# A clamp on GpSimd with another second operation, its subtraction moved into VectorE's product, and a new written-out order on all engines

## The chip, the cores and the metric

One NeuronCore of a Trainium2 chip runs the whole program. The metric is device time in microseconds, from the launch to the end of the program.

## The reference

Input `x` is (4, 64, 24, 24). Two layers follow, each on `gn(x)` (group norm with 32 groups of 2 channels) and each added to `x`. The layers' `w_off`, `w_def` are 3x3 convolution weights.

```python
x = x + deform(gn(x), w_off, b_off, w_def, b_def)                 # layer 0
x = x + relu_groupnorm1(modulated_deform(gn(x), ...))             # layer 1
# deform: offset = conv3x3(x, w_off) + b_off        (2 numbers for each of 9 taps and each pixel)
py = base_y + ky + off_y ; px = base_x + kx + off_x
val = corner(y0, x0, wy0*wx0) + corner(y0, x0+1, wy0*wx1) \
    + corner(y0+1, x0, wy1*wx0) + corner(y0+1, x0+1, wy1*wx1)     # bilinear sample, per tap
out = einsum('bckhw,ock->bohw', val, w_def) + b_def
# layer 1 has a third number for each tap, a mask: val = val * sigmoid(mask)
```

## The kernel before, in words

The four images are two pairs. A *stage* `m` is one layer of one pair: stages 0 and 1 are layer 0 of pairs 0 and 1, stages 2 and 3 are layer 1 of the same pairs. Stage `m + 2` needs all of stage `m`; the two pairs are independent, so that one pair's arithmetic can fill the other's waits. Each stage has nine taps, and a *tap* `n = 9 m + t` (0 to 35) is the unit of the middle of a stage. A bilinear weight is a product of two tents, (min(|dx|, 1) - 1) times (min(|dy|, 1) - 1), and the sample is a small matrix product of such weights with 8x8 windows of the image.

The work of a stage, by the names that the order lists use:
- `stats`, `aggr` (VectorE), `norm` (TensorE), `group` (VectorE), `pow` (GpSimd), `normed` (VectorE): the group norm, written into `xpad`. `band` (GpSimd) copies `xpad` into `bands`; `win` (TensorE, L905, in two parts) makes the windows and `wc` (ScalarE) copies them to `xw`.
- `conv` (TensorE, L927, nine taps into one PSUM slot): the offsets. `off`, `sig` (ScalarE), `mix`, `clip`, `omax` (VectorE), `high` (ScalarE), `pos` (VectorE, L687): the positions.
- `yd`, `ym` (TensorE), `yabs`, `yh` (ScalarE), `yu`, `ymul`, `yl` (VectorE): the tents of the rows, once in a stage.
- For each tap: `x` (TensorE, L959, four matmuls) spreads the column distances into PSUM; `xabs` (ScalarE, L525) takes the absolute value into one of four `xa` buffers; `clamp` (GpSimd, L448) works on that buffer in place; `y` (TensorE, L972, eight matmuls) spreads the row tents into PSUM; `mul` (VectorE, L737) multiplies `xa` with `y`'s PSUM into the weights `s`.
- `v` (TensorE, L990, seven parts): weights times windows; it waits until the last `mul` of its stage is done. `vc` copies `v` out, by ScalarE or VectorE. `w` (TensorE, L1006, nine taps): the second convolution, which waits for all copies of its stage.
- Layer 0 ends with `mid` (VectorE, L750, residual and statistics), layer 1 with `sum`, `last`, `fmean`, `fm`, `fspread`, `fv`, `fvar`, `fpow`, `fscale`, `relu`, `fsum` and the store of `res`.
- `far` and `flag` test whether any offset is too large for the short way; a general way exists behind a branch, and the branch is read at the end of the list.

Nothing schedules at run time: `PE_ORDER`, `DVE_ORDER`, `ACT_ORDER` and `POOL_ORDER` are written-out lists, and each engine runs its list in order, waiting on semaphores. Behind an `@` in `PE_ORDER` stands the PSUM slot (0 to 3) of a job; the slot must have been read by its consumers before the next job writes it, and `xabs` of tap `n` waits for `mul` of tap `n - 4`, which frees its `xa` buffer.

In the lists before, `clip.1` stands ahead of `mul.6`, `x.9` ahead of the last parts of `v.0`, `conv.2` and then all of `v.1` behind `y.17`, and at the end all of `x.18` to `y.35` comes ahead of `v.2`, `v.3`, `w.2` and `w.3`. On GpSimd, `band.1` stands behind `clamp.1`.

Of the kernel before, what the change touches and what calls it, by code (L numbers as in the profile page):

```python
# [62 lines left out]


PE_ORDER = """
norm.0@0 conv.0.0@1 conv.0.1 conv.0.2 conv.0.3 conv.0.4 conv.0.5 conv.0.6 conv.0.7 conv.0.8 win.0.0@2
win.0.1@3 yd.0.0@0 yd.0.1@1 x.0@2 x.1@3 norm.1@0 x.2@2 x.3@0 x.4@3 y.0@1 conv.1.0@2 conv.1.1 y.1@1
conv.1.2 conv.1.3 x.5@0 conv.1.4 conv.1.5 conv.1.6 conv.1.7 conv.1.8 y.2@3 y.3@1 y.4@0 y.5@2 x.6@3 x.7@1
x.8@3 y.6@0 y.7@1 y.8@2 win.1.0@3 v.0.0@0 yd.1.0@1 yd.1.1@2 v.0.1@3 v.0.2@0 v.0.3@1 x.9@2 v.0.4@3
v.0.5@0 v.0.6@2 y.9@1 win.1.1@3 w.0.0@0 w.0.1 w.0.2 w.0.3 w.0.4 w.0.5 w.0.6 w.0.7 w.0.8 x.10@2 x.11@1  # L70
y.10@3 y.11@2 x.12@1 x.13@0 norm.2@1 x.14@3 x.15@0 y.12@2 y.13@1 y.14@3 y.15@0 x.16@2 x.17@1 y.16@2
y.17@3 conv.2.0@1 conv.2.1 conv.2.2 conv.2.3 conv.2.4 conv.2.5 conv.2.6 conv.2.7 conv.2.8 v.1.0@0
v.1.1@2 v.1.2@3 v.1.3@1 v.1.4@0 v.1.5@2 v.1.6@3 win.2.0@1 w.1.0@0 w.1.1 w.1.2 yd.2.0@2 w.1.3 w.1.4 w.1.5
w.1.6 w.1.7 w.1.8 yd.2.1@3 ym.2.0@1 x.18@2 x.19@3 ym.2.1@1 win.2.1@2 norm.3@3 x.20@0 y.18@1 y.19@2
x.21@3 x.22@0 x.23@1 y.20@3 conv.3.0@0 conv.3.1 conv.3.2 conv.3.3 conv.3.4 conv.3.5 conv.3.6 conv.3.7
conv.3.8 win.3.0@2 win.3.1@1 y.21@3 yd.3.0@0 yd.3.1@2 ym.3.0@1 y.22@3 y.23@0 ym.3.1@2 x.24@1 x.25@3
x.26@1 x.27@0 y.24@3 y.25@1 y.26@2 y.27@0 x.28@3 x.29@1 x.30@3 x.31@2 flag@1 y.28@0 y.29@3 y.30@1 y.31@2
x.32@0 x.33@3 x.34@0 x.35@1 y.32@3 y.33@2 y.34@0 y.35@1 v.2.0@3 v.2.1@2 v.2.2@0 v.2.3@3 v.2.4@1 v.2.5@2
v.2.6@0 v.3.0@3 v.3.1@1 v.3.2@2 v.3.3@0 v.3.4@3 v.3.5@1 w.2.0@2 w.2.1 v.3.6@0 w.2.2 w.2.3 w.2.4 w.2.5
w.2.6 w.2.7 w.2.8 w.3.0@3 w.3.1 w.3.2 w.3.3 fm.0@1 w.3.4 w.3.5 fv.0@0 w.3.6 w.3.7 w.3.8 fm.1@2 fv.1@1  # L80
"""

DVE_ORDER = """
stats.0.0 stats.0.1 aggr.0 group.0 stats.1.0 normed.0 stats.1.1 aggr.1 clip.0 omax.0 pos.0 yu.0.0
group.1 yl.0.0 normed.1 yu.0.1 mul.0 yl.0.1 mul.1 mul.2 mul.3 mul.4 mul.5 clip.1 mul.6 mul.7 mul.8 pos.1
omax.1 vc.0.0 yu.1.0 yu.1.1 vc.0.2 vc.0.3 yl.1.0 yl.1.1 vc.0.6 mul.9 mid.0.0 mid.0.1 aggr.2 mul.10
mul.11 group.2 mul.12 mul.13 mul.14 mul.15 normed.2 mul.16 mul.17 vc.1.0 mix.2 clip.2 omax.2 vc.1.4
vc.1.5 pos.2 yu.2.0 mid.1.0 ymul.2.0 mid.1.1 yu.2.1 aggr.3 ymul.2.1 yl.2.0 yl.2.1 group.3 mul.18
normed.3 mul.19 mul.20 mix.3 clip.3 omax.3 oall pos.3 mul.21 yu.3.0 yu.3.1 ymul.3.0 mul.22 mul.23 yl.3.0
ymul.3.1 mul.24 mul.25 mul.26 mul.27 yl.3.1 far mul.28 mul.29 mul.30 mul.31 mul.32 mul.33 mul.34 mul.35  # L90
vc.2.2 vc.2.4 vc.2.6 vc.3.1 vc.3.3 last.0.0 last.0.1 fmean.0 fspread.0 fvar.0 fscale.0 fsum.0 last.1.0
last.1.1 fmean.1 fspread.1 fvar.1 fscale.1 fsum.1
"""

ACT_ORDER = """
off.0 high.0 wc.0.0 wc.0.1 yabs.0.0 xabs.0 yh.0.0 xabs.1 yabs.0.1 xabs.2 yh.0.1 xabs.3 xabs.4 xabs.5
off.1 xabs.6 xabs.7 xabs.8 high.1 wc.1.0 yabs.1.0 yabs.1.1 vc.0.1 yh.1.0 yh.1.1 xabs.9 vc.0.4 vc.0.5
wc.1.1 xabs.10 xabs.11 xabs.12 xabs.13 xabs.14 xabs.15 xabs.16 xabs.17 off.2 sig.2 vc.1.1 vc.1.2 vc.1.3
high.2 vc.1.6 wc.2.0 yabs.2.0 yabs.2.1 xabs.18 xabs.19 yh.2.0 yh.2.1 wc.2.1 xabs.20 xabs.21 xabs.22
xabs.23 off.3 sig.3 high.3 wc.3.0 wc.3.1 yabs.3.0 yabs.3.1 yh.3.0 xabs.24 xabs.25 xabs.26 xabs.27 yh.3.1  # L100
xabs.28 xabs.29 xabs.30 xabs.31 xabs.32 xabs.33 xabs.34 xabs.35 vc.2.0 vc.2.1 vc.2.3 vc.2.5 vc.3.0
vc.3.2 vc.3.4 vc.3.5 vc.3.6 sum.2.0 sum.2.1 relu.0 sum.3.0 sum.3.1 relu.1
"""
# [1038 lines left out]
```

## Time and profile before

| | |
|---|---|
| median of 3 runs | 174.35 us (172.06 to 175.23) |
| the profiled execution | 174.54 us |
| its span | 172.7 us |
| mean granted TensorE clock | 0.84 of full |
| busy: TensorE / GpSimd / VectorE / ScalarE | 118.5 / 87.9 / 75.8 / 63.9 us |

The span is the time between the first and last instruction that the profiler saw; 1.84 us of the profiled execution lie outside it. The busy time of TensorE counts matmuls that overlap in the array by their modelled ends, so that it is no measure of how full the array is. "Start to start" below is the time from one instruction's begin to the next one's on the same engine when neither waits.

### The profile page before, as it was taken

What the parts mean: (1) busy time and instruction counts of PE and PEld (TensorE: products, weight loads), DVE (VectorE), ACT (ScalarE), POOL (GpSimd) and SP (SyncE); (2) the same over time, 40 slices, a digit from 0 to 9 for tenths busy, and PEclk for the clock granted to TensorE, in tenths of its full rate; (3) what the DMA queues carried; (4) which work ended last, traced back from release to release, by engine and by line L of the source; (5) the groups of instructions that cost most, each with busy time, mean ns of one, the idle gap of its engine ahead of it and who ended that gap; (6) DMA issues with size and microseconds to landing.
All of it is one profiled execution on the core that took longest, in us unless ns stands there. A gap on an engine that the chain in (4) does not pass through costs nothing.

```text
span 172.7 us, 4571 instructions
## 1 busy us (share of the span) xinstructions
PE 118.5 (69%) x1953; PEld 77.0 (45%) x1953; DVE 75.8 (44%) x144; ACT 63.9 (37%) x101; POOL 87.9 (51%) x64
## 2 busy tenths in 40 slices
PE   0279949861999836379999858875353769999310
...
POOL 8030099998013199990000699619999980000110
PEclk9999996999579975557999999996555599999965
...
GB/s 169 353 193 4 0 0 4 0 4 0 4 0 6 0 4 0 2 4 0 0 4 4 0 6 0 4 0 4 0 0 0 0 4 0 6 4 4 42 30 78
...
## 3 DMA queue, kind: packets, MB, share of 16 engines
...
## 4 chain that ended last, share of the span: by engine, by line
PE 41%; POOL 40%; issue 6%; DVE 4%; ACT 3%; DMA 3%; ACTq 1%; POOLq 0%; DVEq 0%
POOL xa L448 37%; PE ps L990 14%; PE ps L1006 10%; PE ps L927 8%; PE ps L905 5%; DMA full_m<-c_full 3%; ACT xa L525 1%; POOL rstd L438 1%; POOL bands L396 1%; PE ps L939 1%; DVE s L737 1%; ACT ya L506 1%; DVE xpad L665 1%; PE ps L921 1%; ACT res L544 1%
## 5 line engine op out<-in xcount | busy, mean ns | idle before, releaser
L448 POOL TENSOR_SCALAR xa<-xa 128x576 f32<-128x576 f32 x36 | 76.8, 2155 | 49.7 <-ACT xa L525 49.7
L737 DVE TENSOR_TENSOR s<-xa,ps 128x576 f32<-128x576 f32 x36 | 26.9, 753 | 36.4 <-POOL xa L448 31.1
L525 ACT ACTIVATE xa<-ps 128x576 f32<-128x576 f32 x36 | 22.6, 648 | 28.4 <-PE ps L959 20.9
L990 PE MATMUL ps<-s,xw 64*64 64x228 f32 (+5 forms) x480 | 27.6, 380 | 5.9 <-DVE s L737 5.9
L927 PE MATMUL ps<-xpad,w_o 64*64 64x288 f32 x288 | 25.1, 506 | 0.0
L990 PEld LDWEIGHTS ps<-s,xw 64*64 64x64 f32 x480 | 18.4, 142 | 14.3 <-DVE s L737 5.6
L959 PE MATMUL ps<-pos,soon 64*64 64x288 f16 x144 | 11.4, 339 | 12.7 <-DVE s L737 10.7
L533 ACT ACTIVATE val<-ps 128x504 f32<-128x504 f32 (+5 forms) x23 | 15.7, 724 | 11.3 <-PE ps L990 11.1
L972 PE MATMUL ps<-yh,soon 64*64 64x288 f16 x144 | 13.8, 364 | 8.2 <-DVE s L737 7.2
L1006 PE MATMUL ps<-val,w_d 64*64 64x288 f32 x288 | 19.3, 409 | 0.0
L927 PEld LDWEIGHTS ps<-xpad,w_o 64*64 64x64 f32 x288 | 15.4, 171 | 7.5 <-issue 5.1
L384 DVE COPY val<-ps 128x504 f32<-128x504 f32 (+5 forms) x17 | 12.5, 772 | 10.3 <-PE ps L990 10.2
L972 PE MATMUL ps<-yl,soon 64*64 64x288 f16 x144 | 14.0, 360 | 0.0
L905 PE MATMUL ps<-full_m,bands 128*64 128x64 f32 x400 | 13.0, 223 | 1.4 <-POOL bands L396 1.4
L905 PEld LDWEIGHTS ps<-full_m,bands 128*64 128x64 f32 x400 | 12.1, 138 | 3.3 <-POOL bands L396 2.0
L959 PEld LDWEIGHTS ps<-pos,soon 64*64 64x64 f16 x144 | 5.1, 109 | 18.9 <-issue 18.3
L1006 PEld LDWEIGHTS ps<-val,w_d 64*64 64x64 f32 x288 | 10.6, 132 | 5.7 <-issue 0.2
L443 POOL TENSOR_TENSOR fin<-fin,minus_half 128x1 f32<-128x1 f32 x2 | 1.1, 555 | 23.1 <-DVE fin L787 23.1
L972 PEld LDWEIGHTS ps<-yh,soon 64*64 64x64 f16 x144 | 5.9, 125 | 12.8 <-issue 11.9
L499 ACT ACTIVATE xw<-ps 128x1024 f32<-128x1024 f32 (+1 forms) x8 | 6.5, 830 | 3.5 <-PE ps L905 3.5
L474 ACT ACTIVATE off<-ps,vec 128x576 f32<-128x576 f32 x2 | 1.7, 830 | 15.4 <-PE ps L927 15.4
L477 ACT ACTIVATE off<-ps,vec 128x576 f32<-128x576 f32 x2 | 1.5, 741 | 15.4 <-PE ps L927 15.4
...
## 6 DMA issues: line engine op xcount, KB each, us to landing
...
```

Source lines behind the costliest of these rows:

```text
L384: eng_copy(val[m % 2][:, :, top:end, left:right], src).then_inc(frees("v", m, j), 1)
L448: nc.gpsimd.tensor_scalar(v, v, 1.0, 1.0, ALU.min, ALU.subtract).then_inc(xu_ready, 1)
L499: nc.scalar.activation(v[:, a:a + n], src[:, 0:n], ACT.Copy).then_inc(frees("win", m, g), 1)
L525: nc.scalar.activation(xa[:, n % XA_BUFS, :, :], both(("x", n)), ACT.Abs).then_inc(frees("x", n), 1)
L533: return nc.scalar.activation(to, src, ACT.Copy)
L737: nc.vector.tensor_tensor(s[m % 2][:, :, at:at + 9 * (ROWS - 1) + 1:9, b:b + W], xa[:, n % XA_BUFS, :, :].rearrange("p h (r c) -> p h r c" ...
L905: last = mm(ps[64 * i:64 * i + 64, b + at // 8, Q * (at % 8):Q * (at % 8) + Q], pixel, ident[:, 64 * i:64 * i + 64], start=True, stop=True)
L927: last = mm(ps[64 * h:64 * h + 64, b + i, 0:HALF], w_o[l][64 * i:64 * i + 64, t, :], xpad[m % 2][64 * i:64 * i + 64, rows, c:c + W], start ...
L959: last = mm(ps[64 * i:64 * i + 64, b + h, 0:HALF], ex[64 * h:64 * h + 64, t, :], pos[m % 2][64 * h:64 * h + 64, i, :], start=True, stop=True)
L972: last = mm(ps[64 * i:64 * i + 64, b + h, 0:HALF], sel[64 * h:64 * h + 64, g, :], tent[m % 2][64 * h:64 * h + 64, tile, :], start=part == ...
L990: last = mm(to, xw[m % 2][64 * i:64 * i + 64, GRID * row + w, :], s[m % 2][64 * i:64 * i + 64, h, top:end, a:c], start=True, stop=True)
L1006: last = mm(ps[64 * i:64 * i + 64, b + h, 0:HALF], w_d[l][64 * h:64 * h + 64, t, :], v[:, at:at + 9 * (ROWS - 1) + 1:9, c:c + W], start=t ...
```

## The change

- `clamp` on GpSimd was `min(v, 1) - 1`, one instruction with the operations (min, subtract). It becomes `max(min(v, 1), 0)`, one instruction with (min, max) on the same buffer. `v` is an absolute value, so that the max with 0 alters nothing, and the subtraction is missing from `xa`.
- `mul` on VectorE was one `tensor_tensor` over both halves of a tap (128x576). It becomes two `scalar_tensor_tensor` over 128x288 each, `(xa - 1) * y`, with the constant 1.0 as the scalar. Only the second raises the semaphore that frees the PSUM slot.
- All four lists are new (of PE_ORDER and DVE_ORDER the old lines are left out below, of ACT_ORDER all lines). In the new lists, `norm.1` stands inside `conv.0`; `pow.1` and `band.1` stand ahead of `clamp.0`; `conv.1` starts ahead of `yd.0`; `clip.1` stands behind `mul.8`; `x.9` behind `w.0.0`; `v.1` is put between the taps of `conv.2`; `win.1.0`, `win.2.1` and `win.3.0` stand ahead of a `v`; `v.2` stands between the taps of stages 2 and 3; `w.2.0` to `w.2.5` stand ahead of `v.3`; `flag` and `far` stand behind `w.3`.

```diff
 PE_ORDER = """
...
+norm.0@0 conv.0.0@1 conv.0.1 conv.0.2 conv.0.3 norm.1@2 conv.0.4 conv.0.5 conv.0.6 conv.0.7 conv.0.8
+win.0.0@3 conv.1.0@0 conv.1.1 conv.1.2 yd.0.0@2 yd.0.1@1 x.0@3 conv.1.3 x.1@2 conv.1.4 conv.1.5 conv.1.6
+conv.1.7 x.2@3 conv.1.8 x.3@2 x.4@1 y.0@3 y.1@2 y.2@0 y.3@3 x.5@1 x.6@2 x.7@0 y.4@1 y.5@2 x.8@3 y.6@0
+y.7@1 y.8@3 win.0.1@2 win.1.0@0 v.0.0@1 v.0.1@2 v.0.2@3 v.0.3@0 yd.1.0@1 v.0.4@2 v.0.5@3 v.0.6@0
+yd.1.1@1 win.1.1@2 w.0.0@3 x.9@0 x.10@1 w.0.1 w.0.2 y.9@0 w.0.3 y.10@1 w.0.4 x.11@2 w.0.5 y.11@0 w.0.6
+w.0.7 x.12@1 x.13@2 w.0.8 x.14@0 x.15@1 x.16@2 x.17@0 y.12@1 norm.2@3 y.13@1 y.14@3 y.15@2 y.16@1 y.17@0
+conv.2.0@3 conv.2.1 conv.2.2 conv.2.3 conv.2.4 conv.2.5 v.1.0@2 v.1.1@1 v.1.2@0 v.1.3@2 v.1.4@1 v.1.5@0
+v.1.6@2 conv.2.6 conv.2.7 conv.2.8 w.1.0@1 w.1.1 w.1.2 w.1.3 w.1.4 w.1.5 w.1.6 w.1.7 w.1.8 win.2.0@0
+yd.2.0@2 yd.2.1@3 ym.2.0@1 norm.3@0 ym.2.1@2 x.18@3 x.19@0 x.20@3 x.21@1 x.22@0 x.23@3 conv.3.0@2
+conv.3.1 conv.3.2 y.18@1 conv.3.3 conv.3.4 conv.3.5 y.19@1 conv.3.6 y.20@0 conv.3.7 y.21@1 conv.3.8
+y.22@3 x.24@0 x.25@1 x.26@3 y.23@2 y.24@0 y.25@1 y.26@2 win.2.1@3 win.3.0@0 v.2.0@1 v.2.1@3 v.2.2@2
+x.27@0 yd.3.0@1 yd.3.1@3 v.2.3@0 ym.3.0@2 ym.3.1@1 v.2.4@3 x.28@2 x.29@0 v.2.5@1 x.30@2 win.3.1@3 y.27@0
+y.28@1 y.29@3 x.31@0 x.32@2 x.33@1 y.30@0 v.2.6@3 y.31@2 x.34@1 x.35@0 y.32@3 y.33@2 y.34@1 y.35@0
+w.2.0@3 w.2.1 w.2.2 w.2.3 w.2.4 w.2.5 v.3.0@2 v.3.1@1 v.3.2@0 v.3.3@2 v.3.4@1 v.3.5@0 v.3.6@2 w.2.6
+w.2.7 w.2.8 w.3.0@1 w.3.1 w.3.2 w.3.3 w.3.4 w.3.5 w.3.6 w.3.7 w.3.8 fm.0@0 flag@2 fv.0@3 fm.1@0 fv.1@2
 """
...
 DVE_ORDER = """
...
+stats.0.0 stats.0.1 aggr.0 group.0 stats.1.0 normed.0 stats.1.1 aggr.1 group.1 normed.1 clip.0 omax.0
+pos.0 yu.0.0 yu.0.1 yl.0.0 yl.0.1 mul.0 mul.1 mul.2 mul.3 mul.4 mul.5 mul.6 mul.7 mul.8 clip.1 omax.1
+pos.1 vc.0.0 vc.0.2 vc.0.4 yu.1.0 vc.0.6 yu.1.1 yl.1.0 yl.1.1 mul.9 mul.10 mul.11 mid.0.0 mid.0.1 aggr.2
+mul.12 group.2 mul.13 normed.2 mul.14 mul.15 mul.16 mul.17 vc.1.1 vc.1.3 vc.1.6 mix.2 clip.2 omax.2
+pos.2 mid.1.0 mid.1.1 aggr.3 yu.2.0 group.3 yu.2.1 ymul.2.0 normed.3 ymul.2.1 yl.2.0 yl.2.1 mul.18
+mul.19 mul.20 mul.21 mul.22 mix.3 mul.23 mul.24 mul.25 mul.26 clip.3 omax.3 oall pos.3 vc.2.0 vc.2.2
+yu.3.0 yu.3.1 ymul.3.0 ymul.3.1 vc.2.4 yl.3.0 mul.27 mul.28 mul.29 yl.3.1 mul.30 mul.31 mul.32 mul.33
+mul.34 mul.35 vc.3.1 vc.3.3 vc.3.6 last.0.0 last.0.1 fmean.0 fspread.0 far last.1.0 fvar.0 last.1.1
+fmean.1 fscale.0 fspread.1 fvar.1 fsum.0 fscale.1 fsum.1
 """
...
 POOL_ORDER = """
-pow.0 band.0 clamp.0 pow.1 clamp.1 band.1 clamp.2 clamp.3 clamp.4 clamp.5 clamp.6 clamp.7 clamp.8
-clamp.9 clamp.10 clamp.11 clamp.12 clamp.13 pow.2 clamp.14 clamp.15 clamp.16 clamp.17 band.2 clamp.18
-clamp.19 pow.3 clamp.20 clamp.21 clamp.22 band.3 clamp.23 clamp.24 clamp.25 clamp.26 clamp.27 clamp.28
-clamp.29 clamp.30 clamp.31 clamp.32 clamp.33 clamp.34 clamp.35 fpow.0 fpow.1
+pow.0 band.0 pow.1 band.1 clamp.0 clamp.1 clamp.2 clamp.3 clamp.4 clamp.5 clamp.6 clamp.7 clamp.8
+clamp.9 clamp.10 clamp.11 clamp.12 clamp.13 clamp.14 clamp.15 pow.2 clamp.16 clamp.17 band.2 pow.3
+clamp.18 clamp.19 band.3 clamp.20 clamp.21 clamp.22 clamp.23 clamp.24 clamp.25 clamp.26 clamp.27
+clamp.28 clamp.29 clamp.30 clamp.31 clamp.32 clamp.33 clamp.34 clamp.35 fpow.0 fpow.1
 """
...
@@ -445,7 +445,7 @@
             def clamp(n):
                 wait_taken(pool, "x", n)
                 v = xa[:, n % XA_BUFS, :, :]
-                nc.gpsimd.tensor_scalar(v, v, 1.0, 1.0, ALU.min, ALU.subtract).then_inc(xu_ready, 1)
+                nc.gpsimd.tensor_scalar(v, v, 1.0, 0.0, ALU.min, ALU.max).then_inc(xu_ready, 1)
 
             def band(m):
                 band_copy(pool, nc.gpsimd.tensor_copy, m)
@@ -732,12 +732,11 @@
                         wait_full(dve, *after_value(m - 2))
                 dve.wait_ge(xu_ready, n + 1)
                 wait_full(dve, "y", n)
-                a, b = divmod(t, 3)
-                at = 6 * a + b
-                nc.vector.tensor_tensor(
-                    s[m % 2][:, :, at:at + 9 * (ROWS - 1) + 1:9, b:b + W],
-                    xa[:, n % XA_BUFS, :, :].rearrange("p h (r c) -> p h r c", c=W),
-                    both(("y", n)).rearrange("p h (r c) -> p h r c", c=W), ALU.mult).then_inc(frees("y", n), 1)
+                for h in range(2):
+                    ins = nc.vector.scalar_tensor_tensor(
+                        out=weights_at(s[m % 2], h, t), in0=pixels(xa[:, n % XA_BUFS, h, :]), scalar=1.0,
+                        in1=pixels(ps[:, bank(("y", n), h), 0:HALF]), op0=ALU.subtract, op1=ALU.mult)
+                ins.then_inc(frees("y", n), 1)
 
             def values(m, j):
                 wait_full(dve, "v", m, j)
```

## Rows read from the trace of the kernel before

**Rows 1.** The page: busy time by engine, and the span in 40 slices, in tenths.

```profile
PE 118.5 (69%) x1953; PEld 77.0 (45%) x1953; DVE 75.8 (44%) x144; ACT 63.9 (37%) x101; POOL 87.9 (51%) x64
...
PE   0279949861999836379999858875353769999310
...
POOL 8030099998013199990000699619999980000110
PEclk9999996999579975557999999996555599999965
```

**Rows 2.** The chain of work that ended last: by line, then pieces (start, length, what).

```profile
by line: POOL xa L448 36.9%; PE ps L990 14.2%; PE ps L1006 9.8%; PE ps L927 8.1%; issue 6.0%; PE ps L905 5.5%; DMA full_m<-c_full 2.8%; ACT xa L525 1.5%; POOL rstd L438 1.2%; POOL bands L396 1.2%; PE ps L939 0.9%; DVE s L737 0.9%; ACT ya L5
...
27.81 14.69 POOL xa L448 x7
...
116.04 23.63 POOL xa L448 x11
```

**Rows 3.** Groups by form: line, engine, shapes, count | busy us, mean ns | idle before.

```profile
L448 POOL TENSOR_SCALAR xa<-xa 128x576 f32<-128x576 f32 x36 | 76.8, 2155 | 49.7 <-ACT xa L525 49.7
L737 DVE TENSOR_TENSOR s<-xa,ps 128x576 f32<-128x576 f32 x36 | 26.9, 753 | 36.4 <-POOL xa L448 31.1 <-PE ps L972 5.3
...
L525 ACT ACTIVATE xa<-ps 128x576 f32<-128x576 f32 x36 | 22.6, 648 | 28.4 <-PE ps L959 20.9 <-DVE s L737 7.3
...
L396 POOL COPY bands<-xpad 128x960 f32<-128x960 f32 x4 | 4.4, 1110 | 0.7 <-DVE xpad L665 0.7
...
L750 DVE SCALAR_TENSOR_TENSOR x_mid<-ps,vec,x_l 128x288 f32<-128x288 f32 x4 | 2.0, 511 | 6.6 <-PE ps L1006 6.6
...
L717 DVE TENSOR_TENSOR ya<-ps,ya 128x288 f32<-128x288 f32 x2 | 0.9, 452 | 0.0
```

**Rows 4.** TensorE in order of time: start, length, line, operation, count [idle before].

```profile
9.89 7.15 PE L927 MATMUL ps<-xpad,w_o 64*64 64x288 f32 x72
...
54.04 4.68 PE L1006 MATMUL ps<-val,w_d 64*64 64x288 f32 x72
...
74.31 0.45 PE L921 MATMUL ps<-first 64*64 64x288 f16 x4 [2.00 <-DVE xpad L665]
...
81.57 5.98 PE L990 MATMUL ps<-s,xw 64*64 64x399 f32 x120
87.48 2.09 PE L905 MATMUL ps<-full_m,bands 128*64 128x64 f32 x64
...
95.21 0.73 PE L959 MATMUL ps<-pos,soon 64*64 64x288 f16 x8
...
96.90 1.27 PE L905 MATMUL ps<-full_m,bands 128*64 128x64 f32 x36
...
99.27 0.32 PE L972 MATMUL ps<-yh,soon 64*64 64x288 f16 x4
99.39 0.32 PE L972 MATMUL ps<-yl,soon 64*64 64x288 f16 x4
...
102.62 4.64 PE L927 MATMUL ps<-xpad,w_o 64*64 64x288 f32 x72
...
159.25 1.71 PE L1006 MATMUL ps<-val,w_d 64*64 64x288 f32 x24
```

**Rows 5.** VectorE in order of time: start, length, line, operation, count [idle before].

```profile
19.23 0.82 DVE L687 SCALAR_TENSOR_TENSOR pos<-off,vec,hs 128x576 f16<-128x576 f32 x1
...
32.72 2.17 DVE L737 TENSOR_TENSOR s<-xa,ps 128x576 f32<-128x576 f32 x3 [3.14 <-PE ps L972]
...
42.53 0.75 DVE L737 TENSOR_TENSOR s<-xa,ps 128x576 f32<-128x576 f32 x1 [1.34 <-POOL xa L448]
...
60.75 0.21 DVE L625 BATCH_NORM_AGGREGATE chan<-bn 128x2 f32<-128x12 f32 x1
...
122.92 0.75 DVE L737 TENSOR_TENSOR s<-xa,ps 128x576 f32<-128x576 f32 x1 [1.34 <-POOL xa L448]
...
141.80 0.76 DVE L737 TENSOR_TENSOR s<-xa,ps 128x576 f32<-128x576 f32 x1 [1.34 <-POOL xa L448]
```

More of the change, by code:

```diff
@@ L65 @@
 PE_ORDER = """
[L66 to L80, printed above, removed]
+norm.0@0 conv.0.0@1 conv.0.1 conv.0.2 conv.0.3 norm.1@2 conv.0.4 conv.0.5 conv.0.6 conv.0.7 conv.0.8
@@ L81 @@
+x.27@0 yd.3.0@1 yd.3.1@3 v.2.3@0 ym.3.0@2 ym.3.1@1 v.2.4@3 x.28@2 x.29@0 v.2.5@1 x.30@2 win.3.1@3 y.27@0
+y.28@1 y.29@3 x.31@0 x.32@2 x.33@1 y.30@0 v.2.6@3 y.31@2 x.34@1 x.35@0 y.32@3 y.33@2 y.34@1 y.35@0
+w.2.0@3 w.2.1 w.2.2 w.2.3 w.2.4 w.2.5 v.3.0@2 v.3.1@1 v.3.2@0 v.3.3@2 v.3.4@1 v.3.5@0 v.3.6@2 w.2.6
+w.2.7 w.2.8 w.3.0@1 w.3.1 w.3.2 w.3.3 w.3.4 w.3.5 w.3.6 w.3.7 w.3.8 fm.0@0 flag@2 fv.0@3 fm.1@0 fv.1@2
 """
 DVE_ORDER = """
-stats.0.0 stats.0.1 aggr.0 group.0 stats.1.0 normed.0 stats.1.1 aggr.1 clip.0 omax.0 pos.0 yu.0.0
@@ L85 @@
[L85 to L89, printed above, removed]
@@ L90 @@
-ymul.3.1 mul.24 mul.25 mul.26 mul.27 yl.3.1 far mul.28 mul.29 mul.30 mul.31 mul.32 mul.33 mul.34 mul.35
-vc.2.2 vc.2.4 vc.2.6 vc.3.1 vc.3.3 last.0.0 last.0.1 fmean.0 fspread.0 fvar.0 fscale.0 fsum.0 last.1.0
-last.1.1 fmean.1 fspread.1 fvar.1 fscale.1 fsum.1
+stats.0.0 stats.0.1 aggr.0 group.0 stats.1.0 normed.0 stats.1.1 aggr.1 group.1 normed.1 clip.0 omax.0
+pos.0 yu.0.0 yu.0.1 yl.0.0 yl.0.1 mul.0 mul.1 mul.2 mul.3 mul.4 mul.5 mul.6 mul.7 mul.8 clip.1 omax.1
+pos.1 vc.0.0 vc.0.2 vc.0.4 yu.1.0 vc.0.6 yu.1.1 yl.1.0 yl.1.1 mul.9 mul.10 mul.11 mid.0.0 mid.0.1 aggr.2
@@ L93 @@
+fmean.1 fscale.0 fspread.1 fvar.1 fsum.0 fscale.1 fsum.1
 """
 ACT_ORDER = """
[L96 to L100, printed above, removed]
```

9 lines of the change are left out of this document (7 added, 2 removed).

## The prediction

> **What bounds the kernel now.** I read the page's slices first. TensorE has more busy time than GpSimd (118.5 against 87.9 us), yet its digits fall to 3 and 5 just where GpSimd's stand at 9, and the granted clock falls there too [rows 1]. So the busy shares don't answer the question, and I went to the chain of waits. It does: 36.9% of the span, 63.7 us, is the clamp of L448, in runs such as 7 clamps in 14.69 us and 11 in 23.63 us, 2.10 and 2.15 us apiece; TensorE's own lines come in between such runs [rows 2]. The groups by form show the rest of a tap: 0.648 us on ScalarE, 0.753 on VectorE, and VectorE waited 31.1 us for the clamp [rows 3]. While taps run the clamp sets the pace; between them TensorE does. Last I followed TensorE and VectorE in order of time and noted where stages begin and end; the sum below is made along these marks [rows 4, 5].
>
> **The clamp.** 36 instructions of 2155 ns, of which the trace has no (min, max) form. From below it is bounded by what GpSimd needs to read and write a float at all: the copy of 960 elements took 1110 ns, 1.16 ns each, which for 576 is 0.67 us. From above the nearest row is the present clamp, 2.16 us, 3.74 ns an element, and a max that costs more than a subtraction can't be excluded by any row, so that the upper end lies open [rows 3]. The present clamp takes 3.2 times the copy's time per element, so it isn't moving data that holds it but its arithmetic, and the arithmetic is what the edit alters. One of two operations is kept, so a mere halving of the arithmetic part would give (2.16 + 0.67)/2 = 1.4 us, and if the subtraction is the slow one, near 0.7. I take 1.0 us: two comparisons need no addition, and below about 0.95 us it is hidden behind VectorE anyway. That is a judgement between far ends, and the largest risk in the forecast.
>
> The Trainium skill, "GPSIMD Engine Reference", has two rules here. Its performance section says that a body of at most two operations is bound by the ports at 1.03 cycles an element; that would be an estimated 0.49 us for 576 elements, and the 2.155 us of the clamp disagree. Its section on pitfalls says that a dependent chain of fp32 additions or multiplications pays 4 cycles an element and a compare-and-select body 2.03; by these estimates the clamp is 1.92 us before, which the trace nearly bears out, and 0.97 us after.
>
> **The product.** One instruction of 753 ns becomes two of 288 elements. The nearest rows are the `scalar_tensor_tensor` of L750, same size, PSUM and SBUF in, 511 ns, and the `tensor_tensor` of L717 at the same size, 452 ns [rows 3]. So a pair is 0.90 to 1.02 us. Instructions that follow without a wait overlap a little: three products of 753 took 2.17 us, about 0.04 us less for each [rows 5]. I take 0.95 us. Of 0.2 us x 36 = 7 us more work on VectorE none was on the chain before, since VectorE waited 1.34 us in each tap; with a clamp of 1.0 us this cover is gone, and VectorE and GpSimd go in step at about 1.0 us a tap. ScalarE's 0.65 us and TensorE's x and y (0.12 + 0.24 us at full clock, since two rows of four matmuls each begin 0.12 us apart, at 99.27 and 99.39 [rows 4]) lie beside that. Four `xa` buffers hold a tap for about 0.65 + 1.0 + 0.95 plus semaphores = 2.8 us, 0.7 us a tap, so they don't bind.
>
> The Trainium skill speaks against halves: "VectorE: DVE Perf Modes", section on the TRN2 errata, charges 120 cycles to each instruction with a PSUM source. By its formula a pair is an estimated 0.85 us and the single one 0.725; the row of 0.753 agrees within 4%.
>
> **The order, with the sum along the marks.** Full-clock costs of TensorE: conv 4.64 us (7.15 at half clock), the two parts of win 2.09 and 1.27, v 5.98, w 4.7 [rows 4].
> - *Start to the end of tap 8.* Before it ends at 43.3 [rows 5]. Now `norm.1` inside `conv.0` costs 0.5, which makes positions ready at 20.5 instead of 20.05 [rows 5]; yd, the row tents and `conv.1` ahead of `y.0` bring the first product to about 26.3. Nine taps at 1.0 end at 35.3. Gain 8.0.
> - *To the start of v.0.* It followed at once. Now `win.0.1` and `win.1.0` stand between, 3.4 us of which TensorE can do 1.3 before tap 8 ends: loss 2.1, at 37.4.
> - *v.0 to the end of w.0.* Before 43.3 to 58.7, 15.4 us [rows 4, 5]. Now 6.0 + 1.3 + 4.7 with 0.5 of yd and 1.1 of three x and y, some waiting for slots 0.5: 14.1, at 51.5. Gain 1.3.
> - *w.0 to conv.2.* Before 58.7 to 74.3, 15.6 us, nearly all GpSimd's [rows 4]. Now 2.2 us for `mid` and `aggr.2` (as 58.7 to 60.96 [rows 4, 5]), 0.6 each for norm, group, pow and normed with two products among them, and a slot that `mul.14` frees: 6.3 us, at 57.8. Gain 9.3.
> - *conv.2 to the first taps of stage 2.* Before 74.3 to 95.2, 20.9 us [rows 4]. All of conv.2, v.1, w.1 and `win.2.0` is still there, 4.6 + 6.0 + 4.7 + 2.1 at full clock, with csel, yd, ym and the copy of `win.2.0` 2.2: 19.6, at 77.4. Gain 1.3, half of the clock's 2.5 us in conv.2.
> - *To the end of tap 26.* Before 95.2 to 123.7, 28.5 us, of which 9 clamps, a pow, a band copy and conv.3 [rows 4, 5]. Now norm.3 and the row tents lead to a first product at 83 (5.6), conv.3 paces two products (1.6), the other seven and mix.3 take 7.9 and waits 1.2: 16.3, at 93.7. Gain 12.2.
> - *To the end of tap 35.* Before 18.9 us, nine clamps [rows 5]. Now the positions and row tents of stage 3 come behind `mul.26`, with v.2 beside them: 7.4 us, then nine taps at 1.0 and 0.9 for yl and slots: 17.3, at 111.0. Gain 1.6.
> - *To the end of w.3.* Before 142.6 to 161.0, 18.4 us, v and w of both stages less what TensorE had begun [rows 4, 5]. Now 2.0 us of w.2 left, v.3 6.0, three taps of w.2 1.6, w.3 4.9: 14.5, at 125.5. Gain 3.9.
> - *The tail.* Before 161.0 to 172.7, 11.7 us [rows 4]. `flag`, `far` and `fsum.0` now stand ahead of `fscale.1`: 0.3 more.
>
> Gains 8.0 + 1.3 + 9.3 + 1.3 + 12.2 + 1.6 + 3.9 = 37.6, losses 2.1 + 0.3 = 2.4: 172.7 - 35.2 = 137.5 us. With the 1.84 us outside the span 139.3; the profiled execution is within 0.2 us of the median, so no correction. I add 0.7 us for half clock at places where TensorE waits for taps: **140 us**. What is late next is TensorE, in the blocks of conv, v and w, and VectorE inside the taps. The waits that the change adds are `clip.1` behind `mul.8` (stage 1's positions, which nobody needs before `yd.1.0`, some 3 us later) and `far` (only the branch at the end waits for it); both cost nothing here. `band.1` ahead of `clamp.0` is covered, since `clamp.0` waits for `xabs.0` until 23.
>
> **Rivals.** *The clamp costs what it did*, since its time does not depend on which two operations it holds. The Trainium skill's rule of 1.03 cycles for any body of up to two operations ("GPSIMD Engine Reference", performance section) has that shape, if not that size. For the rival: no row shows GpSimd's cost by operation. Against: 3.2 times the copy. Along the same marks, with 2.13 us a tap: tap 8 ends at 43, conv.2 begins near 70, the marks of 77 and 93.7 become 89 and 111, tap 35 ends at 135.5, w.3 at 148, the end at 160, 162 with what lies outside. That is still below now, by v.2 and half of w.2 between the clamps instead of behind them. Clumsy meetings in the new order could eat that: 157 to 174.
> *A half gain*, a clamp of 1.3 to 1.7 us: GpSimd stays the pace in the taps. Each 0.1 us above 1.0 adds about 2 to 3 us over 36 taps, partly hidden: 147 to 156.
> *Slower*: max costs more than the subtraction. At 2.13 us the sum is 162, and with GpSimd the sole pace each 0.1 us more adds 3.6 us; it is slower than 177.8 us from a clamp of 2.6 us on, and at 3.0 us it gives 193. For it only that no row excludes it.
> *The order misses*: with the fast clamp, TensorE's list stalls on slots, as `conv.2` on `mul.14` and `y.0` on `conv.1`, and each stall is followed by half clock, 2.5 us for a conv [rows 4]. Four such places give 150.
>
> **Chances.** Forecast 0.60 (133 to 147, from a product of 0.85 to 1.02 us, which is 36 x 0.1 = 4 us down and 3 up, and slips of the marks); order misses 0.11 (150); half gain 0.10 (151); clamp unchanged 0.15 (162); slower 0.04 (193). The range runs from 131 to 160: it leaves out half of the unchanged clamp, the slower one and the edges of the others. A measurement here can tell about 2% from no change, 170.9 to 177.8 us. Unchanged clamps reach into that with a third of their 0.15: faster 0.91, same 0.05, slower 0.04.
>
> **What would show it.** L448's mean near 1.0 us (right below 1.1, half gain from 1.3, wrong at 2.1); L737 as 72 instructions of 0.45 to 0.51 us; the chain with L448 below 10% and L990, L1006 and L927 at its head; the product of tap 8 ended by 36, conv.2 begun by 59, w.3 ended by 127; the clock above 0.84. The forecast is wrong if GpSimd's digits still stand at 9 through the taps, or if TensorE shows long idle pieces ahead of y or v with both other engines free.

## The result and the profile after

| | before | after |
|---|---|---|
| median | 174.0 us (172.06 to 175.23, 4 runs) | 136.22 us (135.89 to 138.45, 4 runs) |
| ratio, 95% interval | | 0.785 (0.776 to 0.794) |
| profiled execution, its span | 174.54, 172.7 | 136.41, 134.6 |
| granted TensorE clock | 0.84 | 0.949 |

The forecast was 140 us (131 to 160). Run again later, the changed kernel gave 135.32 us (134.57 to 135.97). The ratio leaves out the changed kernel's execution of 138.45 us, which ran over 1.5% above the fastest. The granted clock is a mean that counts the start of the program as full clock, because the trace has no clock record there; the section on the halves shows that TensorE ran at the lower of its two levels in that stretch.

The page after, with busy time and the slices, answers to [rows 1]:

```profile
PE 107.7 (80%) x1953; PEld 76.7 (57%) x1953; DVE 78.2 (58%) x181; ACT 62.8 (47%) x100; POOL 37.1 (28%) x64
...
PE   0029999979999987899999879799997899995200
...
POOL 8222130555000356600000096250154700001300
PEclk9999999999999998569999999999999999999955
```

GpSimd lost 50.8 us of busy time. TensorE does the same 1953 matmuls, and its digits stand at 7 to 9 from the fourth slice until the tail. The chain of waits, by line, beside [rows 2]:

```profile
by line: PE ps L989 17.4%; PE ps L1005 13.2%; PE ps L926 12.2%; PE ps L904 9.4%; issue 7.5%; PE ps L971 5.9%; DVE s L736 5.7%; ACT xa L525 5.1%; DMA x_l<-x 4.7%; PE ps L958 2.1%; POOL xa L448 1.0%; PE ps L941 0.9%; POOLq L227 0.9%; DVE yl L
```

The clamp, 36.9% before, is at 1.0% (1.3 us); v, w, conv and win now head the chain. The groups by form, beside [rows 3]:

```profile
L736 DVE SCALAR_TENSOR_TENSOR s<-xa,ps 128x288 f32<-128x288 f32 x72 | 27.4, 447 | 6.0 <-POOL xa L448 3.1 <-PE ps L971 2.9
L448 POOL TENSOR_SCALAR xa<-xa 128x576 f32<-128x576 f32 x36 | 25.2, 714 | 39.5 <-ACT xa L525 39.4
...
L525 ACT ACTIVATE xa<-ps 128x576 f32<-128x576 f32 x36 | 22.0, 651 | 11.6 <-DVE s L736 7.3 <-PE ps L958 4.2
```

A clamp takes 714 ns where it took 2155. The 72 half products, 27.4 us in total, cost nearly what the 36 whole ones did (26.9). VectorE's wait for the clamp fell from 31.1 to 3.1 us. TensorE in order of time, as [rows 4]:

```profile
10.19 4.08 PE L926 MATMUL ps<-xpad,w_o 64*64 64x288 f32 x32
...
15.12 2.71 PE L926 MATMUL ps<-xpad,w_o 64*64 64x288 f32 x40
...
35.18 3.54 PE L989 MATMUL ps<-s,xw 64*64 64x399 f32 x48
...
55.86 0.48 PE L920 MATMUL ps<-first 64*64 64x288 f16 x4
56.10 4.76 PE L926 MATMUL ps<-xpad,w_o 64*64 64x288 f32 x48
...
76.66 0.55 PE L958 MATMUL ps<-pos,soon 64*64 64x288 f16 x8
...
110.22 6.06 PE L989 MATMUL ps<-s,xw 64*64 64x399 f32 x120
115.99 6.22 PE L1005 MATMUL ps<-val,w_d 64*64 64x288 f32 x96
```

and VectorE, as [rows 5]:

```profile
26.62 3.00 DVE L736 SCALAR_TENSOR_TENSOR s<-xa,ps 128x288 f32<-128x288 f32 x8 [0.82 <-POOL xa L448]
30.04 3.73 DVE L736 SCALAR_TENSOR_TENSOR s<-xa,ps 128x288 f32<-128x288 f32 x10 [0.42 <-PE ps L971]
...
87.50 3.00 DVE L736 SCALAR_TENSOR_TENSOR s<-xa,ps 128x288 f32<-128x288 f32 x8
...
106.07 3.00 DVE L736 SCALAR_TENSOR_TENSOR s<-xa,ps 128x288 f32<-128x288 f32 x8 [0.17 <-PE ps L971]
...
129.16 0.76 DVE L802 TENSOR_TENSOR res<-res,x_mid 128x576 f32<-128x576 f32 x1 [0.94 <-ACT res L544]
```

Eight half products in a row take 3.00 us, 0.375 us from start to start and 0.75 us a tap. Along the marks of the prediction:

| stretch | before, us | forecast | measured |
|---|---|---|---|
| start to end of tap 8 | 43.3 | 35.3 | 33.8 |
| to v.0 | 0 | 2.1 | 1.4 |
| v.0 to end of w.0 | 15.4 | 14.1 | 14.0 |
| w.0 to conv.2 | 15.6 | 6.3 | 6.7 |
| conv.2 to x.18 | 20.9 | 19.6 | 20.8 |
| to end of tap 26 | 28.5 | 16.3 | 13.8 |
| to end of tap 35 | 18.9 | 17.3 | 18.6 |
| to end of w.3 | 18.4 | 14.5 | 13.1 |
| tail | 11.7 | 12.0 | 12.4 |

(After: ends of tap 8, 26 and 35 at 33.8, 90.5 and 109.1; w.0 ends at 49.2, w.3 at 122.2.)

### The profile page after: what moved, and what is told of

It reads as the page before. It is cut to its first block, busy times and chain, and to the rows that moved or that the text cites. A ratio compares the mean times of both kernels' runs of the same rounds, so it can differ in the third digit from the quotient of the medians.

```text
span 134.6 us, 4607 instructions
## 1 busy us (share of the span) xinstructions
PE 107.7 (80%) x1953; PEld 76.7 (57%) x1953; DVE 78.2 (58%) x181; ACT 62.8 (47%) x100; POOL 37.1 (28%) x64
## 4 chain that ended last, share of the span: by engine, by line
PE 64%; DVE 9%; ACT 7%; issue 7%; DMA 5%; POOL 1%; SPq 1%; POOLq 1%; ACTq 0%; DVEq 0%
PE ps L989 17%; PE ps L1005 13%; PE ps L926 12%; PE ps L904 9%; PE ps L971 6%; DVE s L736 6%; ACT xa L525 5%; DMA x_l<-x 5%; PE ps L958 2%; POOL xa L448 1%; PE ps L941 1%; POOLq L227 1%; DVE yl L724 1%; ACT xw L499 1%; PE ps L938 1%
## 5 line engine op out<-in xcount | busy, mean ns | idle before, releaser
L448 POOL TENSOR_SCALAR xa<-xa 128x576 f32<-128x576 f32 x36 | 25.2, 714 | 39.5 <-ACT xa L525 39.4
L736 DVE SCALAR_TENSOR_TENSOR s<-xa,ps 128x288 f32<-128x288 f32 x72 | 27.4, 447 | 6.0 <-POOL xa L448 3.1
L989 PE MATMUL ps<-s,xw 64*64 64x84 f32 (+5 forms) x480 | 25.1, 355 | 0.2 <-ACT xa L525 0.2
L384 DVE COPY val<-ps 128x294 f32<-128x294 f32 (+5 forms) x18 | 13.2, 760 | 15.5 <-PE ps L989 15.5
L926 PEld LDWEIGHTS ps<-xpad,w_o 64*64 64x64 f32 x288 | 13.3, 153 | 5.2 <-issue 2.8
L1005 PEld LDWEIGHTS ps<-val,w_d 64*64 64x64 f32 x288 | 14.8, 132 | 1.6 <-issue 0.5
L971 PE MATMUL ps<-yh,soon 64*64 64x288 f16 x144 | 12.0, 316 | 3.0 <-ACT xa L525 1.1
L971 PE MATMUL ps<-yl,soon 64*64 64x288 f16 x144 | 12.0, 305 | 0.0
L438 POOL TENSOR_TENSOR rstd<-gvar,minus_half 128x1 f32<-128x1 f32 x4 | 2.2, 551 | 30.2 <-DVE gvar L634 30.2
L892 PE MATMUL ps<-chan,full_m 128*128 128x2 f32 x8 | 1.9, 305 | 6.9 <-DMA full_m<-c_full 6.6
```

What stands on the lines that cost most here:

```text
L384: eng_copy(val[m % 2][:, :, top:end, left:right], src).then_inc(frees("v", m, j), 1)
L448: nc.gpsimd.tensor_scalar(v, v, 1.0, 0.0, ALU.min, ALU.max).then_inc(xu_ready, 1)
L736: ins = nc.vector.scalar_tensor_tensor(out=weights_at(s[m % 2], h, t), in0=pixels(xa[:, n % XA_BUFS, h, :]), scalar=1.0, in1=pixels(ps[:, ...
L926: last = mm(ps[64 * h:64 * h + 64, b + i, 0:HALF], w_o[l][64 * i:64 * i + 64, t, :], xpad[m % 2][64 * i:64 * i + 64, rows, c:c + W], start ...
L971: last = mm(ps[64 * i:64 * i + 64, b + h, 0:HALF], sel[64 * h:64 * h + 64, g, :], tent[m % 2][64 * h:64 * h + 64, tile, :], start=part == ...
L989: last = mm(to, xw[m % 2][64 * i:64 * i + 64, GRID * row + w, :], s[m % 2][64 * i:64 * i + 64, h, top:end, a:c], start=True, stop=True)
```

## The experiments

**What each part is worth.** Two kernels cross the two parts of the change: the operations of clamp and product on one side, all four lists on the other.

```diff
 # old_order_new_ops: the lists of before, and
-                nc.gpsimd.tensor_scalar(v, v, 1.0, 1.0, ALU.min, ALU.subtract).then_inc(xu_ready, 1)
+                nc.gpsimd.tensor_scalar(v, v, 1.0, 0.0, ALU.min, ALU.max).then_inc(xu_ready, 1)
 # with the product by halves
 # new_order_old_ops: the new lists, clamp and product of before
```

> The old lists with the new clamp (min, max) and the product by halves. If the clamp's price is the cause and the order only collects it: L448 near 0.7 us, 138 to 150 us, ratio to before 0.79 to 0.86, since TensorE's list still puts v.2, v.3, w.2 and w.3 (18.4 us) behind the last tap. If the order is the cause: 160 to 172 us.

Measured: 143.34 us (142.85 to 144.91), ratio 0.824 (0.817 to 0.831).

> The new lists with the old clamp (min, subtract) and the single product. By the prediction's rival 'the clamp costs what it did': 162 us (157 to 174), L448 at 2.13 us. If the new order is only good for a fast clamp: 174 us or more.

Measured: 163.79 us (163.19 to 166.04), ratio 0.937 (0.930 to 0.943); L448 at 2147 ns. From about 174.4 us, the operations alone (fast clamp and halves) give 31.0 us and the lists alone 10.6; together they give 38. On top of the operations the lists are worth 7.1 us (143.34 to 136.22). The rival "the clamp costs what it did" had been priced at 162 us along the marks, and this kernel is that case: 1.8 us off. That the order must come with a fast clamp to be of use is refuted.

**The halves.**

```diff
 # new_order_old_clamp_halves: new lists, clamp (min, subtract)
-                        ... scalar=1.0, ... op0=ALU.subtract, op1=ALU.mult)
+                        ... scalar=0.0, ... op0=ALU.subtract, op1=ALU.mult)
 # new_kernel_single_product: new lists and clamp (min, max), and
-   two scalar_tensor_tensor, (xa - 1) * y over 128x288 each
+   one tensor_tensor, xa * y over 128x576
```

> As new_order_old_ops, but the product by halves, with 0.0 in place of 1.0 as the scalar to subtract, since the clamp has subtracted already. If the halves cost only where VectorE has no cover: within 1.5 us of new_order_old_ops, because VectorE waits more than 1 us in each tap for the clamp. If each half's fixed price comes through anyway: 4 to 7 us slower.

Measured: 166.96 us (166.21 to 167.51), ratio 0.955: 3.17 us slower than new_order_old_ops, between both expectations. The two traces say where. TensorE in conv.0 with the halves:

```profile
10.47 4.08 PE L926 MATMUL ps<-xpad,w_o 64*64 64x288 f32 x32
...
15.43 4.43 PE L926 MATMUL ps<-xpad,w_o 64*64 64x288 f32 x40
```

and without them:

```profile
9.38 3.99 PE L927 MATMUL ps<-xpad,w_o 64*64 64x288 f32 x32
...
13.84 2.71 PE L927 MATMUL ps<-xpad,w_o 64*64 64x288 f32 x40
```

The last 40 matmuls of conv.0 took 4.43 against 2.71 us, and conv.0 began 1.1 us later. The first product begins at 28.65 against 25.33 us. From there to the end of the last product it is 112.25 us with the halves and 112.45 without: they cost nothing where a product runs. The 3.3 us arise ahead of any product. The later begin is a load's: VectorE waited 1.51 us for `x_l` of the second pair, and 0.28 us without the halves.

The rest, 2.2 us, is TensorE's clock. Matmuls of conv.0 start every 0.120 us at first and every 0.060 us later, and in 13 of the 14 traces of this case the change falls together with the trace's first clock record, which says full clock: at 19.1 us with the halves, at 13.2 without them, at 15.0 in the changed kernel, at 15.1 in the kernel before. Ahead of it there is no record, and the views then print 1.00. In the fourteenth, mended_and_warm (below), the records begin ahead of conv.0, and there they say 0.5 from 9.2 to 12.6 us, while matmuls start every 0.120 us, and full clock from 12.6 us on, where the starts go to 0.060. So the slow start is the level of 1.2 GHz. Loads are not its cause: from 12 to 15 us the traces show 0 GB/s, and with the halves the slow pace went on until 19.1. Why the clock rose 6 us later in one execution than in the other stays open; in both TensorE had worked without a pause since conv.0 began.

> The new kernel with the product as one tensor_tensor over both halves; the subtraction of 1 is left out. In the changed kernel eight half products took 3.00 us, 0.75 us a pair, against 0.70 to 0.72 us for a single one: so 0.5 to 1.5 us faster than the changed kernel. If the pair cost 0.95 us as the prediction had it: 4 us faster or more.

Measured: 136.19 us, scattered from 132.79 to 138.47, with no ratio to lean on. In the profiled executions it is 80.51 us from the first product's start to the last one's end, against 82.45 and 81.92 in two of the changed kernel. (The 103.3 and 101.3 us that two expectations below give for this stretch reach to the end of VectorE's last instruction, L802.) The clock was low at other places in the three, which blurs this. Within the four runs of nine taps alone, each from its first product's start to its last one's end, the single product saves 1.25 us against new_kernel_again. So the halves cost about 1.3 us here by one profile each, within what was expected.

**Is GpSimd hidden, and up to what price?** A memset on an idle buffer ahead of each clamp lengthens a tap on GpSimd and changes no other instruction.

```diff
+                nc.gpsimd.memset(pad[:, n % 16, :], 0.0)     # 128x300 f16 (clamp_1us); 128x900, n % 5 (clamp_1p5us)
                 v = xa[:, n % XA_BUFS, :, :]
```

> The new kernel with a memset of 128x300 f16 (about 0.33 us) on an idle buffer ahead of each clamp, so that a tap takes GpSimd about 1.0 us instead of 0.67. By the prediction's cover (below VectorE's pace it is hidden), with VectorE's measured pace of 0.75 us: 1 to 5 us slower, as 0.25 us comes out in some of the 36 taps. If GpSimd is fully hidden: no change. Fully on the path: 12 us.

> The same with a memset of 128x900 f16 (about 0.85 us), so that GpSimd takes about 1.5 us a tap. By the prediction's slope of 2 to 3 us for each 0.1 us above VectorE's pace: 7.5 times 2 to 3, less what waits anyway, 12 to 20 us slower than the changed kernel. If TensorE's blocks hide most of it: under 8 us.

GpSimd in order of time, in clamp_1us:

```profile
29.19 0.35 POOL L448 MEMSET pad<- 128x300 f16 x1
29.50 0.67 POOL L450 TENSOR_SCALAR xa<-xa 128x576 f32<-128x576 f32 x1
30.11 0.35 POOL L448 MEMSET pad<- 128x300 f16 x1
```

and in clamp_1p5us:

```profile
28.70 0.66 POOL L450 TENSOR_SCALAR xa<-xa 128x576 f32<-128x576 f32 x1
29.31 0.84 POOL L448 MEMSET pad<- 128x900 f16 x1
30.12 0.66 POOL L450 TENSOR_SCALAR xa<-xa 128x576 f32<-128x576 f32 x1
```

Start to start a tap takes 0.92 and 1.42 us. The times are 136.82 us (135.3 to 138.3) and 143.35 us (142.84 to 144.63), ratios 0.788 (0.781 to 0.795) and 0.823 (0.816 to 0.830). With the kernels above this is a curve for the same lists: 136.2 us at 0.64 us a tap, 136.8 at 0.92, 143.35 at 1.42, 167.0 at 2.10 (that one with 3.3 us of its own in the head). Up to 0.92 us a clamp is hidden, as far as a spread of 1 to 2 us between executions lets one see. From there to 1.42 each 0.1 us costs 1.3 us. From 1.42 to 2.10 it is 3.5, or 3.0 without the 3.3 us of the head; all 36 taps would make 3.6.

**Why (min, max) is fast.** One kernel, seven forms of the instruction, on the same buffers and the same shape.

```diff
-                nc.gpsimd.tensor_scalar(v, v, 1.0, 0.0, ALU.min, ALU.max).then_inc(xu_ready, 1)
+                FORMS[FORM[n % 7]](v).then_inc(xu_ready, 1)     # FORM = (0, 1, 2, 3, 4, 5, 6)
```

> The new kernel with seven pairs of operations in the clamp, tap n taking form n mod 7: (min, subtract), (min, max), (max, min), min alone, (min, add -1), (min, mult 1), (subtract, min); the product subtracts 1 where the clamp has not. If additions and multiplications are the slow part: the four forms with one of them near 2.1 us, the three with only comparisons near 0.7. If only the pair (min, max) is fast: the other six near 2.1 us. If it goes by the number of operations: min alone fastest, all pairs alike.

The instructions that write the tile `xa`, one line for each form, in the order named; duration min, median, max:

```profile
L448 POOL TENSOR_SCALAR xa<-xa x6: 2137/2140/2154, 23.1 to 126.8; 128x576 f32<-128x576 f32 x6
L449 POOL TENSOR_SCALAR xa<-xa x5: 661/662/980, 25.2 to 115.9; 128x576 f32<-128x576 f32 x5
L450 POOL TENSOR_SCALAR xa<-xa x5: 2132/2133/2139, 26.1 to 116.8; 128x576 f32<-128x576 f32 x5
L451 POOL TENSOR_SCALAR xa<-xa x5: 1650/1653/1654, 28.2 to 118.9; 128x576 f32<-128x576 f32 x5
L452 POOL TENSOR_SCALAR xa<-xa x5: 2131/2138/2138, 29.8 to 120.5; 128x576 f32<-128x576 f32 x5
L453 POOL TENSOR_SCALAR xa<-xa x5: 2130/2137/2277, 31.9 to 122.6; 128x576 f32<-128x576 f32 x5
L454 POOL TENSOR_SCALAR xa<-xa x5: 2137/2142/2143, 34.1 to 124.7; 128x576 f32<-128x576 f32 x5
```

(max, min), the same two comparisons in the other order, takes 2.13 us, and min alone 1.65, more than twice the pair (min, max). The idea that the subtraction is the slow part is refuted. (One execution, 155.69 us; clamp_forms_2 below, 146.49 us.)

> Seven more forms on GpSimd, tap n taking form n mod 7: (min 1, max 0), (min 1, max -1), (min 1, min 1), (mult 1, min 1), max alone, (mult 1, add -1), a plain copy; the clamp at 1 is left out of the last three. If only the pair (min, max) in this order has a short way, whatever its constants: the first two at 0.66 us, the copy near 0.7, max alone at 1.65, the other pairs at 2.13. If other common pairs have one as well: (mult, add) near 0.7 too.

The same view of this kernel, its forms in the order named:

```profile
L448 POOL TENSOR_SCALAR xa<-xa x6: 661/666/668, 24.2 to 116.8; 128x576 f32<-128x576 f32 x6
L449 POOL TENSOR_SCALAR xa<-xa x5: 665/667/1171, 24.8 to 107.3; 128x576 f32<-128x576 f32 x5
L450 POOL TENSOR_SCALAR xa<-xa x5: 2137/2143/2145, 26.9 to 109.7; 128x576 f32<-128x576 f32 x5
L451 POOL TENSOR_SCALAR xa<-xa x5: 2138/2140/2227, 29.0 to 111.8; 128x576 f32<-128x576 f32 x5
L452 POOL TENSOR_SCALAR xa<-xa x5: 1650/1654/1659, 31.1 to 113.9; 128x576 f32<-128x576 f32 x5
L453 POOL TENSOR_SCALAR xa<-xa x5: 668/671/673, 32.7 to 115.5; 128x576 f32<-128x576 f32 x5
L454 POOL COPY xa<-xa x5: 662/664/892, 33.4 to 116.1; 128x576 f32<-128x576 f32 x5
```

Three forms run at the copy's 0.66 us: (min, max) with either constant, and (mult, add). Every other pair takes 2.14 us and a single operation 1.65. The durations would fit short ways for a few pairs and one general way for all else, at 1.65 us with one operation and 0.49 more with a second; that is a reading, and no run looked inside the instruction. Twelve forms of `tensor_scalar` were seen; which other pairs are fast is open.

**Can the order be mended?** Four steps of the new lists that the trace shows waiting were moved.

```diff
-stats.0.0 stats.0.1 aggr.0 group.0 stats.1.0 normed.0 stats.1.1            (DVE; in mended_order alone)
+stats.0.0 stats.0.1 aggr.0 group.0 normed.0 stats.1.0 stats.1.1
-... fvar.1 fsum.0 fscale.1 fsum.1                                          (DVE)
+... fvar.1 fscale.1 fsum.0 fsum.1
-xabs.18 xabs.19 xabs.20 yh.2.0 yh.2.1 xabs.21                              (ACT)
+xabs.18 xabs.19 yh.2.0 xabs.20 yh.2.1 xabs.21
-clamp.18 clamp.19 band.3 clamp.20 clamp.21 clamp.22                        (POOL)
+clamp.18 clamp.19 clamp.20 clamp.21 clamp.22 band.3
```

> The new kernel with four steps moved: normed.0 ahead of stats.1.0 (it waited 0.35 us for the second input's load), fscale.1 ahead of fsum.0 (fpow.1 took 1.12 us beside fsum.0, 0.55 alone), band.3 behind clamp.22 and yh.2.0 behind xabs.19 (yl.2.0 took 1.6 us beside the band copy, 0.75 alone). If these waits are on the path: 0.8 to 1.5 us faster than the changed kernel. If TensorE covers them: within 0.5 us.

Measured: 136.52 us (136.33 to 138.31), ratio 0.786 (0.780 to 0.791), no faster. From the first to the last product it was 80.59 us against 82.45, but the first product began at 28.85 against 26.62. Both differences are mostly the clock's. Its first record, at full clock, is at 19.1 us here against 15.0, and from there to 125 us it stayed full, so that conv.2 to x.18 took 19.1 us against 20.8 with its low stretch. Three more kernels ran beside each other on one chip:

> The changed kernel itself, run again as the measure for the two beside it: 136.2 us (135.5 to 137), first product between 25.3 and 26.7 us from the start, 103.3 us from there to the last product.

> mended_order without its move of normed.0 (three moves left: fscale.1, band.3, yh.2.0). In mended_order the part behind the first product was 2.0 us shorter than in the changed kernel (101.3 against 103.3 us) and the head 2.2 us longer, with all of conv.0 at half pace. If the head's length has to do with the move of normed.0: 134 to 135 us. If the half pace in conv.0 comes with any such kernel: 136 to 137 us, the middle still 101.3 us.

> mended_without_head with 32 small matmuls on zeros ahead of norm.0 and 12 behind it, their results unused. In all runs the first taps of conv.0 go at 0.127 us a matmul and the later ones at 0.068. If TensorE's idleness ahead of conv.0 is the cause: conv.0 takes 5 us in place of 7.8 and the whole is 2 to 3 us faster than mended_without_head. If it is something else, or the matmuls hold norm.0 up: no gain, or a loss up to 1 us.

```diff
+warm.0@3 norm.0@0 warm.1@3 conv.0.0@1 ...        # on top of mended_without_head; warm.0 does not wait for the load of full_m
-WARM = {}
+WARM = {0: 32, 1: 12}
```

Measured: 135.32 us (134.57 to 135.97), ratio 0.781 (0.775 to 0.787); 136.67 us (135.26 to 137.35), ratio 0.786 (0.778 to 0.793); 137.64 us (135.34 to 138.15), ratio 0.793 (0.787 to 0.800). None of the mended kernels beats the changed one. The mend did shorten `yl`. In the changed kernel `yl` of stage 2 and GpSimd's work beside it:

```profile
79.44 2.37 DVE L724 TENSOR_TENSOR yl<-ya,yh 128x576 f16<-128x576 f32 x2 [0.30 <-ACT yh L519]
```

and GpSimd in order of time:

```profile
77.80 1.50 POOL L448 TENSOR_SCALAR xa<-xa 128x576 f32<-128x576 f32 x2
79.25 1.11 POOL L396 COPY bands<-xpad 128x960 f32<-128x960 f32 x1
80.32 2.02 POOL L448 TENSOR_SCALAR xa<-xa 128x576 f32<-128x576 f32 x2
```

and in mended_without_head:

```profile
77.22 1.68 DVE L724 TENSOR_TENSOR yl<-ya,yh 128x576 f16<-128x576 f32 x2
```

`yl` is ready at 78.9 in place of 80.4 us in new_kernel_again, yet the first product of stage 2 came later, at 81.64 against 80.28. TensorE's windows from 78 to 82 us, new_kernel_again first (columns: stretch, length, busy us and count of PE, PEld, DVE, ACT, POOL, granted clock, DMA share, GB/s):

```profile
78.00:82.00 4.00, 4.00 (x76) 2.44 (x72) 3.23 (x5) 1.48 (x3) 2.97 (x4) 1.00 0.01 2
```

and mended_without_head:

```profile
78.00:82.00 4.00, 4.00 (x51) 2.39 (x48) 1.25 (x3) 0.36 (x1) 1.42 (x2) 0.60 0.02 4
```

The second had a granted clock of 0.60 there, so that it stood at 1.2 GHz for most of the stretch; the first three taps of conv.3 took 3.12 us against 1.68. conv.3 began at 77.86 and 77.83 us in the two, behind nearly the same work (2.52 and 2.67 us busy from 74 to 78 us), so no cause can be named for the clock.

The clock would explain that the first product came 1.36 us later, but not where the 1.5 us of `yl` went. mended_order shows that, since it has the same mend of `yl` at full clock (granted clock 1.00 from 74 to 86 us). TensorE and VectorE in new_kernel_again:

```profile
77.95 1.68 PE L926 MATMUL ps<-xpad,w_o 64*64 64x288 f32 x24
...
80.28 0.81 DVE L736 SCALAR_TENSOR_TENSOR s<-xa,ps 128x288 f32<-128x288 f32 x2
```

and in mended_order:

```profile
79.14 1.68 DVE L724 TENSOR_TENSOR yl<-ya,yh 128x576 f16<-128x576 f32 x2
...
79.90 1.68 PE L926 MATMUL ps<-xpad,w_o 64*64 64x288 f32 x24
...
81.97 0.82 DVE L736 SCALAR_TENSOR_TENSOR s<-xa,ps 128x288 f32<-128x288 f32 x2 [1.16 <-PE ps L971]
```

`yl` is ready at 80.8 us there, but VectorE then waits 1.16 us for `y.18`, which stands in `PE_ORDER` behind three taps of conv.3. From conv.3's begin to the first product it is 2.19 us against 2.45: of 1.5 us only 0.26 arrive. And the same mend, `yh.2.0` ahead of `xabs.20`, made `x.23` and so conv.3 wait 0.79 us for ScalarE in place of 0.30. From x.18 to the first product it is 5.24 us with the mend and 5.07 without. So the mend of stage 2 gained nothing even at full clock.

The warm-up matmuls raised the clock, but not for conv.0. The page of mended_and_warm, in slices of 3.34 us:

```profile
PE   6739999879999976899999679899997899998200
...
PEclk9986999999999999599999968999999999999755
```

Its clock records say full clock from 5.8 to 9.2 us, half from 9.2 to 12.6 and full again. TensorE stood idle from 7.5 to 9.6 us, between the last warm-up matmul and conv.0, and in that gap the clock fell. So conv.0 began at 1.2 GHz here as well, and its first 32 matmuls went in 3.51 us against 3.77. Whether matmuls in the gap would have kept the clock was not tried.

## Why the prediction held, and where it did not

*What bounds the kernel.* Right: the clamp's pace set the taps, and with it gone TensorE heads the chain.

*The clamp at 1.0 us.* Mis-sized, 0.67 us at the median (0.71 with waits for VectorE), at the low end of the range given. The reason behind the choice failed: "two comparisons need no addition" does not hold, as (max, min) takes 2.13 us and (mult, add) 0.67. The comparison with the copy showed that there was room; it did not show which operations would use it. The estimate from the Trainium skill ("GPSIMD Engine Reference", the section on pitfalls: 4 cycles for dependent fp32 additions, 2.03 for comparisons) fitted the old clamp by chance: (max, min), without an addition, takes as long. Its rule of 1.03 cycles in the performance section, an estimated 0.49 us, is a quarter below the 0.66 us of the three fast forms and far from the others. The error had little consequence, since clamp_1us gives nearly the same time at 0.92 us a tap. That (min, max) is one of the fast pairs was luck: had (max, min) been written, the same reasoning would have given the same forecast, and the clamp would have cost 2.13 us.

*The product at 0.95 us.* Mis-sized: 0.75 us. The rows chosen as nearest carried a pointer scalar (511 ns) or none (452 ns), and with the constant it is 447; and a pair overlaps by 0.07 us for each instruction, not 0.04. That made each full run of nine taps about 2 us shorter (7.15 us in stage 0, where 9.0 was forecast), which is most of the 3.2 us by which tap 26 ended ahead of its mark (90.5 against 93.7), 1.5 of them won by tap 8.

*The marks.* The sum came to 137.5 us of span against 134.6, nearer than its parts: the errors of the nine stretches have both signs and partly cancel; their sizes add up to 9.5 us. Two stretches were longer than forecast by over 1 us, conv.2 to x.18 by 1.2 and to tap 35 by 1.3 us. In the first, the clock was the term. The text spoke of half of the clock's 2.5 us, but the sum held conv.2 at its full-clock 4.6 us; in this trace the clock was low from 52.6 to 59.4 us (a 5 and a 6 in the slices), and conv.2 took 6.2 us. The 0.7 us added for the clock was too little for that. Nor is 7.15 us the price of a conv at half clock: in the kernel before, the clock rose in the midst of that conv, at 15.1 us, and 72 matmuls at 0.120 us would be 8.6. In the second, the way from tap 26 to the first product of stage 3 took 10.9 us where 7.4 was forecast, since `win.2.1` (until 92.0 us), six of the seven parts of v.2 and `win.3.1` keep TensorE busy ahead of `y.27`; the nine taps behind it gave 2.2 us of that back. The 0.3 us for the tail were about right.

*The rivals.* "Clamp unchanged", 162 us: measured 163.8. "Half gain": the slope of 2 to 3 us for each 0.1 us holds as a mean over 0.92 to 2.10 us (2.6, or 2.3 without the head's 3.3 us), but it bends, 1.3 and then 3.0 to 3.5. That TensorE's blocks between the taps absorb the first part would explain it; no run separates this. At 1.42 us the result is 143.35, below the 147 to 156 given for that case. "Order misses" showed itself only in the clock at conv.2.
